# Layer 0 of a two-layer transformer kernel: the chain that prepares the FFN input starts half a batch earlier

## The chip, the cores and the metric

One NeuronCore of a Trainium2 chip runs the whole program. The metric is the device time of one execution in microseconds (us). The engines are TensorE (PE: matrix products and transposes; PEld is its weight load), VectorE (DVE), ScalarE (ACT), GpSimd (POOL) and the queues that issue DMAs (SP). Each runs its own instruction list in order, and semaphores are the only thing that ties the lists together.

## The reference

Input `x` is 16 batches x 256 positions x 256 features in fp32. Four steps follow one another, each added to `x`:

```python
x = x + tanh(g_xattn[0]) * L0_xattn(layernorm(x), ctx, ctx)   # decayed running sum of ctx*ctx, times layernorm(x)
x = x + tanh(g_ffn[0])   * L0_ffn(layernorm(x), w_gate, w_up, w_down)
x = x + tanh(g_xattn[1]) * L1_xattn(layernorm(x), ctx, ctx, 16)   # softmax attention with RoPE and ALiBi
x = x + tanh(g_ffn[1])   * L1_ffn(layernorm(x), w_fc, b_fc, w_proj, b_proj)
```

The change touches the first two. `L0_ffn` quantises both operands of every product to FP4 in blocks of 16 along the contracted dimension (scale = max|x|/6, value rounded to the grid 0, 0.5, 1, 1.5, 2, 3, 4, 6, times scale): `gate = q(y) q(Wg)^T`, `up = q(y) q(Wu)^T`, `h = silu(gate) * up`, `out = q(h) q(Wd)^T`, with 256 features and 704 hidden.

## The kernel before

Everything of layer 0 stays in SBUF. A batch is 256 rows, held as 2 tiles of 128 partitions, and each engine runs one `l0_body(b)` for each of the 16 batches (`over_batches`: bodies 0 to 3 and 12 to 15 are written out, 4 to 11 are a hardware loop of two bodies). The order of every engine's list is written by hand in that engine's `l0_body`. The bodies are software-pipelined: body b does the gate/up product of batch b, the down product of batch b-1 (`prv`), the last preparation of batch b+1 (`nxt`), and earlier work of b+2 to b+4 (`nxt2` is b+2).

**The y chain** makes the quantised FFN input of a batch n from the residual `xres` after its first update:
`l0_x_mix` (DVE, `mix`) and `l0_x_sum` (POOL, `xres += mix`); `l0_y_stats` (DVE, mean and variance); `l0_ln_step` (POOL, four tiny operations to `shift`; the same call serves the statistics of batch b+4); `l0_y_norm` (ACT, `yn`); `l0_y_scale` (DVE: maximum of each block L1287, a small scalar operation L1279 and reciprocal L1281, to `yrinv`); `l0_y_scaled` (POOL, `ys`, L1096); `l0_y_magic` (ACT, magnitude `ymag`); `l0_y_round` (DVE, `yup` then `ycode`); `l0_y_quantised` (POOL, `yq`, L1103); `l0_turn_input` (PE, four transposes into PSUM `ps_r`, L471); `l0_input_out` (ACT, `yth`, L837); `l0_y_low` (DVE, `ytl`, L1301).

**The h chain** of batch b: `l0_gate_up` (PE: four units u0 to u3 of 12 matmuls, L491 to L493, into two pairs of banks of `ps_gu`); after each unit `l0_silu` (ACT) and `l0_multiply` (DVE, `h`, L1311; called mul0 to mul3 below). Unit u2 overwrites the banks of u0 and waits for mul0, u3 waits for mul1. Then `l0_hidden_scale` (DVE: L1318, L1279, L1281, to `hrinv`), `l0_hidden_scaled` (POOL, `hs`, L1110), `l0_hidden_magic` (ACT, `hmag`, L866), and in the next body `l0_hidden_up` and `l0_hidden_codes` (DVE, `hup` L1324 and `hcode` L1330) and `l0_hidden_quantised` (POOL, `hq`, L1116), whose result PE transposes in four groups (`l0_turn_hidden`, L510; ACT copies each, `l0_hidden_out`) and multiplies (`l0_down`, L522). `l0_add_ffn` (DVE, L1334) adds the result to the residual.

PE ends a body with `l0_decayed_sum(b+3)` (L460 to L462), which writes `ps_r` as `l0_turn_input` does, so the two take turns with `l0_x_mix` and `l0_y_low`. In body 0 DVE also quantises W_down (`w_scale` to `w_dequant`) and PE transposes it (`turn_w2`).

Of the kernel before, what the change touches and what calls it, by code (L numbers as in the profile page):

```python
# [145 lines left out]
def build_main(nc, load, loaded, out_v, g_xattn, g_ffn, w_gate_up, w_down, w_fc, b_fc, w_proj, b_proj, ident, decay,  # L146
# [3 lines left out]
    with ExitStack() as keep:  # L150
# [262 lines left out]
        def _(pe):  # L413
# [112 lines left out]
            def l0_hidden_out(b, nxt):  # L526
                l0_turn_hidden(b, 0)
                l0_turn_hidden(b, 1)
                l0_down(b, 0)
                l0_turn_hidden(b, 2)  # L530
                l0_down(b, 1)
                if nxt:
                    l0_turn_input(nxt)
                l0_turn_hidden(b, 3)
                l0_down(b, 2)
                l0_down(b, 3)
# [244 lines left out]
        def _(act):  # L781
# [86 lines left out]
            def l0_body(b):  # L868
                prv = b.shifted(-1)
                l0_silu(b, 0)  # L870
                if b.shifted(1):
                    l0_y_norm(b.shifted(1))
                l0_silu(b, 1)
                if b.shifted(3):
                    l0_x_norm(b.shifted(3))
                l0_silu(b, 2)
                if b.shifted(1):
                    l0_y_magic(b.shifted(1))
                l0_silu(b, 3)
                if prv:  # L880
                    l0_hidden_out(prv, 0)
                    l0_hidden_out(prv, 1)
                else:
                    w_magnitude(W2)
                if b.shifted(4):
                    l0_square(b.shifted(4))
                if prv:
                    l0_hidden_out(prv, 2)
                if b.shifted(1):
                    l0_input_out(b.shifted(1))  # L890
                if prv:
                    l0_hidden_out(prv, 3)
                else:
                    for k in range(KH0 // 2):
                        w2_out(k)
                l0_hidden_magic(b)

# [131 lines left out]
            l0_square(fourth)  # L1029
            l0_input_out(first)  # L1030
            over_batches(act, l0_body, L0_AHEAD, L0_BEHIND)

            at_v_of(first)
# [18 lines left out]
        def _(pool):  # L1052
# [66 lines left out]
            def l0_body(b):  # L1119
# [7 lines left out]
                if b.shifted(1):  # L1127
                    l0_y_scaled(b.shifted(1))
                if b.shifted(2):
                    l0_x_sum(b.shifted(2))  # L1130
                if b.shifted(1):
                    l0_y_quantised(b.shifted(1))
                l0_hidden_scaled(b)
                if b.shifted(2):
                    l0_ln_step(b.shifted(4), b.shifted(2))

# [81 lines left out]
            l0_y_scaled(first)  # L1218
            l0_y_quantised(first)
            v_aug_rows = a_v_aug[:, :, :, :, :].rearrange("p a c h s -> p (a c h) s")  # L1220
            nc.gpsimd.memset(v_aug_rows[:, :, HD + 1:2 * HD], 0.0)
# [24 lines left out]
        def _(dve):  # L1246
# [90 lines left out]
            def l0_body(b):  # L1337
# [6 lines left out]
                l0_multiply(b, 0)  # L1344
                if nxt:
                    l0_y_scale(nxt)
                l0_multiply(b, 1)
# [3 lines left out]
                if nxt2:  # L1351
                    l0_x_mix(nxt2)
                l0_multiply(b, 2)
                if b.shifted(4):
                    l0_x_stats(b.shifted(4))
                l0_multiply(b, 3)
                if nxt:
                    l0_y_round(nxt)
                l0_hidden_scale(b)
                if not prv:  # L1360
                    w_up(W2)
                    w_round(W2)
                    w_dequant(W2)
                if nxt:
                    l0_y_low(nxt)
                if nxt2:
                    l0_y_stats(nxt2)
                if prv:
# [279 lines left out]
            for k in range(len(w1_turns)):  # L1648
                if k == 4:
                    l0_y_round(first)  # L1650
                w1_low(k)
            l0_y_low(first)
            over_batches(dve, l0_body, L0_AHEAD, L0_BEHIND)

# [91 lines left out]
```

## Time and profile before

| | |
|---|---|
| three runs, device time | 862.52, 864.06, 865.29 us; median 864.06 |
| the profiled execution | 860.4 us, of which the span from first to last instruction is 858.4 us |
| layer 0 loop over batches | about 46 us to 343 us of the span |
| busy share over the span | PE 82%, DVE 82%, ACT 57%, POOL 52% |
| of the stretch 180 to 220 us (40 us) | PE 37.83, DVE 32.70, ACT 18.93, POOL 26.39 us busy |

Durations come from the one profiled execution. The overlap of two neighbours on one engine is real: an instruction may start up to 0.1 us before the recorded end of the one ahead. "[0.74 <-DVE h L1311]" behind a row is the engine's idle time before that instruction and who ended it.

### The profile page before, as it was taken

The numbers are of one execution on the slowest core, as the hardware profiler recorded it, in microseconds if no ns is written. First come the engines' busy times: TensorE is split into PE (matmuls) and PEld (weight loads), VectorE is DVE, ScalarE is ACT, GpSimd is POOL, SyncE is SP. The second block draws the span as 40 slices with busy tenths as digits, with TensorE's granted clock in tenths as the row PEclk, the third lists the DMA queues.
The fourth block names the chain that finished last, engine by engine and source line by source line (L and its number), as shares of the span: only waits on it lengthen the run. The fifth ranks groups of instructions, "written<-read, shape, count | busy, mean of one in ns | idle before, by whom it ended". The sixth has DMA issues, their size and how long they took to land.

```text
span 858.4 us, 16548 instructions
## 1 busy us (share of the span) xinstructions
PE 708.2 (82%) x5075; PEld 511.9 (60%) x5090; DVE 702.6 (82%) x1230; ACT 487.1 (57%) x939; POOL 445.0 (52%) x331
## 2 busy tenths in 40 slices
PE   2357999999999998779999999999999775777776
PEld 1246888887878876555665655566566443444444
DVE  6767888888878878868888988888888748898985
ACT  3334444544444442328777777777777684555653
POOL 4523666665666545744444455454542525565563
PEclk9877999999999999879999999999999997898999
DMA  8700000000000000010000000000001000010011
GB/s 277 226 26 0 1 1 1 0 0 0 0 0 1 1 1 1 1 48 5 3 2 2 1 1 1 1 1 1 1 1 50 2 2 0 26 37 24 26 37 50
DMA packets 17719, 18.35 MB, mean 21 GB/s; under 512 B 1670, under 2 KB 16912, under 8 KB 17680
## 3 DMA queue, kind: packets, MB, share of 16 engines
q1 hardware_dynamic: 17084, 17.66, 6.3%
q8 instruction: 21, 0.34, 0.2%
q10 hardware_dynamic: 596, 0.20, 0.1%
q14 instruction: 18, 0.15, 0.1%
HBM read 13.39 MB, written 4.19 MB: 20 GB/s over the span
## 4 chain that ended last, share of the span: by engine, by line
PE 44%; DVE 26%; issue 13%; ACT 9%; POOL 4%; DMA 1%; DVEq 1%; ACTq 0%; POOLq 0%; SPq 0%
PE ps_o L522 9%; PE a_ps_t L561 7%; PE a_ps_m L579 6%; DVE maxima L1499 5%; PE a_ps_pv L615 4%; DVE f_ps_small L1584 4%; PE a_ps_s L600 3%; PE ps_gu L491 2%; DVE yscale L1279 2%; DVE f_hcode L1600 2%; PE ps_gu L493 2%; PE ps_gu L492 2%; PE a_ps_pv L623 1%; ACT yn L830 1%; ACT probs L920 1%
## 5 line engine op out<-in xcount | busy, mean ns | idle before, releaser
L1499 DVE TENSOR_REDUCE maxima<-a_ps_m 128x2 f32<-128x512 f32 x256 | 166.4, 686 | 35.4 <-PE a_ps_m L579 34.7
L920 ACT ACTIVATE probs<-a_ps_s 128x512 f32<-128x512 f32 x256 | 149.1, 601 | 42.3 <-PE a_ps_s L600 39.5
L579 PE MATMUL a_ps_m<-stack_t 64*128 64x256 f32 x512 | 107.6, 328 | 19.7 <-DVE maxima L1499 16.6
L579 PEld LDWEIGHTS a_ps_m<-stack_t 64*128 64x128 f32 x512 | 68.2, 188 | 78.6 <-DVE maxima L1499 49.4
L1142 POOL TENSOR_TENSOR stack<-roped,stack 128x512 f32<-128x512 f32 x32 | 42.7, 1334 | 116.9 <-DVE stack L1489 115.4
L600 PE MATMUL a_ps_s<-stack_t 64*128 64x256 f32 x512 | 100.0, 308 | 3.7 <-ACT probs L920 2.8
L522 PE MATMUL ps_o<-w2t,hqt 128*128 128x256 f32 (+1 forms) x384 | 99.1, 392 | 4.6 <-ACT hqt L851 4.6
L491 PE MATMUL ps_gu<-w1h,yth 128*128 128x352 f32 x256 | 87.5, 342 | 14.1 <-DVE h L1311 14.1
L615 PE MATMUL a_ps_pv<-probs,v_aug 128*32 128x256 f32 x1024 | 83.0, 396 | 2.9 <-ACT probs L920 2.5
L911 ACT CAST stack_t<-a_ps_t 128x512 fp32r<-128x512 f32 x128 | 70.9, 588 | 24.7 <-PE a_ps_t L561 23.8
L561 PE MATMUL a_ps_t<-idf,stack 128*128 128x128 f32 x512 | 77.3, 294 | 9.3 <-POOL stack L1142 4.9
L492 PE MATMUL ps_gu<-w1l,yth 128*128 128x352 f32 x256 | 82.7, 323 | 0.0
L493 PE MATMUL ps_gu<-w1h,ytl 128*128 128x352 f32 x256 | 82.5, 322 | 0.0
L522 PEld LDWEIGHTS ps_o<-w2t,hqt 128*128 128x128 f32 (+1 forms) x384 | 66.3, 189 | 25.5 <-issue 13.4
L600 PEld LDWEIGHTS a_ps_s<-stack_t 64*128 64x128 f32 x512 | 68.5, 187 | 12.8 <-ACT probs L920 6.6
L843 ACT ACTIVATE sg<-ps_gu 128x352 f32<-128x352 f32 x64 | 29.7, 465 | 76.6 <-PE ps_gu L493 76.6
L561 PEld LDWEIGHTS a_ps_t<-idf,stack 128*128 128x128 f32 x512 | 58.9, 148 | 22.4 <-ACT stack_t L911 8.2
L1191 POOL TENSOR_TENSOR f_hup<-f_h,f_hmag 128x2048 f32<-128x2048 f32 x16 | 58.3, 3642 | 10.5 <-DVE f_hcode L1600 9.5
L491 PEld LDWEIGHTS ps_gu<-w1h,yth 128*128 128x128 f32 x256 | 48.2, 188 | 20.2 <-DVE h L1311 19.1
L1116 POOL TENSOR_TENSOR hq<-hcode,hscale 128x1408 f32<-128x1408 bf16 x16 | 41.5, 2596 | 35.6 <-DVE hcode L1330 35.6
L981 ACT ACTIVATE f_h<-f_ps_fc 128x512 f32<-128x512 f32 x64 | 36.1, 596 | 37.9 <-POOL f_hup L1191 35.5
L1110 POOL TENSOR_TENSOR hs<-h,hrinv 128x1408 f32<-128x1408 f32 x16 | 42.7, 2668 | 22.9 <-DVE hrinv L1281 22.9
(176 smaller groups left out, 1589.4 us busy)
## 6 DMA issues: line engine op xcount, KB each, us to landing
xres<-in_x SPq DMA_DIRECT2D x16, 256.0 KB, 3.1
ctx<-in_ctx SPq DMA_DIRECT2D x16, 256.0 KB, 4.0
out_x<-f_y SPq DMA_DIRECT2D x16, 256.0 KB, 2.1
w1a_raw<-in_w_gate_up SPq DMA_DIRECT2D x1, 1024.0 KB, 5.9
w_raw<-in_w_fc SPq DMA_DIRECT2D x1, 1024.0 KB, 5.4
w_raw<-in_w_proj SPq DMA_DIRECT2D x1, 1024.0 KB, 5.0
w_raw<-in_w_down SPq DMA_DIRECT2D x1, 704.0 KB, 9.2
stack_t<-neg_max_t SPq DMA_DIRECT2D x32, 8.0 KB
```

The source lines that it names most:

```text
L491: nc.tensor.matmul(into, yth[:, kc, c, :], w1h[:, kc, cols], start=kc == 0, stop=False)
L492: nc.tensor.matmul(into, yth[:, kc, c, :], w1l[:, kc, cols], start=False, stop=False)
L493: ins = nc.tensor.matmul(into, ytl[:, kc, c, :], w1h[:, kc, cols], start=False, stop=kc == KD - 1)
L522: ins = nc.tensor.matmul(ps_o[:, c, :], hqt[0:rows, g, n, :], w2t[0:rows, k, :], start=k == 0, stop=k == KH0 - 1)
L561: ins = nc.tensor.transpose(a_ps_t[:, g % 2, (n * C + c) * P:(n * C + c + 1) * P], a_stack[:, b.par, which, c, 2 * pair:2 * pair + 2, :].r ...
L579: ins = nc.tensor.matmul(a_ps_m[:, half, n, :], a_stack_t[b.par][rows, 0, pair, c * P:(c + 1) * P], a_stack_t[b.par][rows, 1, pair, :], st ...
L600: ins = nc.tensor.matmul(a_ps_s[:, half, n, :], a_stack_t[b.par][rows, 1, pair, kc * P:(kc + 1) * P], a_stack_t[b.par][rows, 0, pair, :], ...
L615: ins = nc.tensor.matmul(a_ps_pv[32 * n:32 * n + 32, quad % 2, 0:T], a_v_aug[:, b.par, kc, 4 * quad + n, :], a_probs[:, (2 * g + n % 2) % ...
L911: nc.scalar.copy(a_stack_t[b.par][:, g % 2, pair:pair + 2, :].rearrange("p a t -> p (a t)"), a_ps_t[:, g % 2, :]).then_inc(a_t, 1)
L920: nc.scalar.activation(a_probs[:, u % 8], a_ps_s[:, u % 2], ACT.Exp).then_inc(a_exp, 1)
L1191: nc.gpsimd.tensor_tensor(f_blocks(f_hup[:, :]), f_blocks(f_h[:, b.par]), f_spread(f_hmag[:, b.par], F_NBH), ALU.add).then_inc(f_g_hup, 1)
L1499: nc.vector.tensor_reduce(a_maxima[:, b.par, c, 4 * quad + half:4 * quad + half + 3:2], a_ps_m[:, half], X, ALU.max).then_inc(a_v_max, 1)
```

## The change

In words, by engine, for body b:

- **VectorE**: `l0_y_scale` goes from behind mul0 (for b+1) to just ahead of `l0_add_ffn` (for b+2). `l0_y_round(b+1)` goes from behind mul3 to behind `l0_x_mix`, ahead of mul2. `l0_y_stats(b+2)` goes from behind `l0_y_low` to behind mul3, ahead of `l0_hidden_scale`.
- **GpSimd**: `l0_y_scaled` goes from behind `hq` (for b+1) to the end of the body (for b+2); `l0_y_quantised(b+1)` goes ahead of `l0_x_sum(b+2)`; `l0_ln_step` goes ahead of `l0_hidden_scaled`.
- **ScalarE**: `l0_y_norm` goes from behind the first silu (for b+1) to ahead of `l0_hidden_magic` (for b+2); `l0_y_magic(b+1)` goes from behind the third silu to the head of the body; `l0_x_norm` and `l0_square` shift by a place; `l0_input_out(b+1)` goes ahead of the third hidden copy.
- **TensorE**: `l0_turn_input(b+1)` goes from behind the second down group to behind the second transpose group.
- Batch 1's norm, scale and scaling, which body 0 did, are now done ahead of the loop.

```diff
--- before.py
+++ after.py
@@ -526,11 +526,11 @@
             def l0_hidden_out(b, nxt):
                 l0_turn_hidden(b, 0)
                 l0_turn_hidden(b, 1)
+                if nxt:
+                    l0_turn_input(nxt)
                 l0_down(b, 0)
                 l0_turn_hidden(b, 2)
                 l0_down(b, 1)
-                if nxt:
-                    l0_turn_input(nxt)
                 l0_turn_hidden(b, 3)
                 l0_down(b, 2)
                 l0_down(b, 3)
@@ -867,32 +867,31 @@
 
             def l0_body(b):
                 prv = b.shifted(-1)
+                if b.shifted(1):
+                    l0_y_magic(b.shifted(1))
                 l0_silu(b, 0)
-                if b.shifted(1):
-                    l0_y_norm(b.shifted(1))
-                l0_silu(b, 1)
                 if b.shifted(3):
                     l0_x_norm(b.shifted(3))
+                l0_silu(b, 1)
                 l0_silu(b, 2)
-                if b.shifted(1):
-                    l0_y_magic(b.shifted(1))
                 l0_silu(b, 3)
                 if prv:
                     l0_hidden_out(prv, 0)
                     l0_hidden_out(prv, 1)
                 else:
                     w_magnitude(W2)
+                if b.shifted(1):
+                    l0_input_out(b.shifted(1))
                 if b.shifted(4):
                     l0_square(b.shifted(4))
                 if prv:
                     l0_hidden_out(prv, 2)
-                if b.shifted(1):
-                    l0_input_out(b.shifted(1))
-                if prv:
                     l0_hidden_out(prv, 3)
                 else:
                     for k in range(KH0 // 2):
                         w2_out(k)
+                if b.shifted(2):
+                    l0_y_norm(b.shifted(2))
                 l0_hidden_magic(b)
 
             def at_v_of(b):
@@ -1028,6 +1027,7 @@
                 w1_high(k)
             l0_square(fourth)
             l0_input_out(first)
+            l0_y_norm(second)
             over_batches(act, l0_body, L0_AHEAD, L0_BEHIND)
 
             at_v_of(first)
@@ -1125,14 +1125,13 @@
                     at_rstd(first)
                     at_q_parts(first)
                 if b.shifted(1):
-                    l0_y_scaled(b.shifted(1))
+                    l0_y_quantised(b.shifted(1))
                 if b.shifted(2):
                     l0_x_sum(b.shifted(2))
-                if b.shifted(1):
-                    l0_y_quantised(b.shifted(1))
+                    l0_ln_step(b.shifted(4), b.shifted(2))
                 l0_hidden_scaled(b)
                 if b.shifted(2):
-                    l0_ln_step(b.shifted(4), b.shifted(2))
+                    l0_y_scaled(b.shifted(2))
 
             def at_low_part(b, which):
 
@@ -1217,6 +1216,7 @@
             l0_ln_step(fourth, second)
             l0_y_scaled(first)
             l0_y_quantised(first)
+            l0_y_scaled(second)
             v_aug_rows = a_v_aug[:, :, :, :, :].rearrange("p a c h s -> p (a c h) s")
             nc.gpsimd.memset(v_aug_rows[:, :, HD + 1:2 * HD], 0.0)
             nc.gpsimd.memset(v_aug_rows[:, :, HD:HD + 1], 1.0).then_inc(a_v_aug_laid, 1)
@@ -1342,29 +1342,27 @@
                     l0_hidden_up(prv)
                     l0_hidden_codes(prv)
                 l0_multiply(b, 0)
-                if nxt:
-                    l0_y_scale(nxt)
                 l0_multiply(b, 1)
                 if not prv:
                     w_scale(W2)
                     w_times(W2)
                 if nxt2:
                     l0_x_mix(nxt2)
+                l0_y_round(nxt)
                 l0_multiply(b, 2)
                 if b.shifted(4):
                     l0_x_stats(b.shifted(4))
                 l0_multiply(b, 3)
-                if nxt:
-                    l0_y_round(nxt)
+                if nxt2:
+                    l0_y_stats(nxt2)
                 l0_hidden_scale(b)
                 if not prv:
                     w_up(W2)
                     w_round(W2)
                     w_dequant(W2)
-                if nxt:
-                    l0_y_low(nxt)
+                l0_y_low(nxt)
                 if nxt2:
-                    l0_y_stats(nxt2)
+                    l0_y_scale(nxt2)
                 if prv:
                     l0_add_ffn(prv)
 
@@ -1650,6 +1648,7 @@
                     l0_y_round(first)
                 w1_low(k)
             l0_y_low(first)
+            l0_y_scale(second)
             over_batches(dve, l0_body, L0_AHEAD, L0_BEHIND)
 
             dve.wait_ge(t_gu, last.count(4, 4))
```

TensorE, body 2, the place between the transposes of the hidden codes and the down product (`yq` is the input that is turned, `hq` the hidden codes):

```order
 L510 MATMUL ps_tb<-idf,hq 128x128 x2
 L510 MATMUL ps_tb<-idf,hq 64x128
-L522 MATMUL ps_o<-w2t,hqt 128x256 x3
-L510 MATMUL ps_ta<-idf,hq 128x128 x3
-L522 MATMUL ps_o<-w2t,hqt 128x256 x3
 L471 MATMUL ps_r<-idf,yq 128x128 x4
+L522 MATMUL ps_o<-w2t,hqt 128x256 x3
+L510 MATMUL ps_ta<-idf,hq 128x128 x3
+L522 MATMUL ps_o<-w2t,hqt 128x256 x3
 L510 MATMUL ps_tb<-idf,hq 128x128 x2
```

The four transposes of `yq` now stand ahead of the first two down groups.

VectorE before, from the hidden rounding of the batch behind to the second multiply pair of body 2 (`h` is a multiply, `yscale` and `yrinv` the y scale, `mix` the x mix):

```order
L1324 SCALAR_TENSOR_TENSOR hup<-hmag,hs 128x1408
L1330 SCALAR_TENSOR_TENSOR hcode<-hmag,hup 128x1408
L1311 TENSOR_TENSOR h<-sg,ps_gu 128x352
L1287 TENSOR_REDUCE yscale<-yn 128x32
L1279 TENSOR_SCALAR yscale<-yscale 128x32
L1281 RECIPROCAL yrinv<-yscale 128x32
L1311 TENSOR_TENSOR h<-sg,ps_gu 128x352
L1269 SCALAR_TENSOR_TENSOR mix<-ps_r,gates,xn 128x512
L1311 TENSOR_TENSOR h<-sg,ps_gu 128x352
L1250 BN_STATS stats<-xres 128x6 x2
L1257 BN_AGGR mv<-stats 128x2 x2
L1311 TENSOR_TENSOR h<-sg,ps_gu 128x352
```

VectorE of the changed kernel, the same place:

```order
L1324 SCALAR_TENSOR_TENSOR hup<-hmag,hs 128x1408
L1330 SCALAR_TENSOR_TENSOR hcode<-hmag,hup 128x1408
L1311 TENSOR_TENSOR h<-sg,ps_gu 128x352 x2
L1269 SCALAR_TENSOR_TENSOR mix<-ps_r,gates,xn 128x512
L1293 SCALAR_TENSOR_TENSOR yup<-ymag,ys 128x512
L1297 SCALAR_TENSOR_TENSOR ycode<-ymag,yup 128x512
L1311 TENSOR_TENSOR h<-sg,ps_gu 128x352
L1250 BN_STATS stats<-xres 128x6 x2
L1257 BN_AGGR mv<-stats 128x2 x2
L1311 TENSOR_TENSOR h<-sg,ps_gu 128x352
L1250 BN_STATS stats<-xres 128x6 x2
```

The y scale no longer stands between the first and the second multiply, the y rounding stands ahead of the third, and a second pair of statistics stands behind the fourth.

GpSimd before, one body from `hq` on (`ys` is the scaled and `yq` the quantised input, `var` to `shift` the ln step, `hs` the scaled hidden):

```order
L1116 TENSOR_TENSOR hq<-hcode,hscale 128x1408
L1096 TENSOR_TENSOR ys<-yn,yrinv 128x512
L1090 TENSOR_TENSOR xres<-xres,mix 128x512
L1103 TENSOR_TENSOR yq<-ycode,yscale 128x512
L1110 TENSOR_TENSOR hs<-h,hrinv 128x1408
L1080 TENSOR_TENSOR var<-mv,eps 128x4
L1082 TENSOR_TENSOR rstd<-var,pow_half 128x4
L1084 TENSOR_TENSOR neg_rstd<-rstd,minus_one 128x4
L1086 TENSOR_TENSOR shift<-mv,neg_rstd 128x4
```

GpSimd of the changed kernel, the same body:

```order
L1116 TENSOR_TENSOR hq<-hcode,hscale 128x1408
L1103 TENSOR_TENSOR yq<-ycode,yscale 128x512
L1090 TENSOR_TENSOR xres<-xres,mix 128x512
L1080 TENSOR_TENSOR var<-mv,eps 128x4
L1082 TENSOR_TENSOR rstd<-var,pow_half 128x4
L1084 TENSOR_TENSOR neg_rstd<-rstd,minus_one 128x4
L1086 TENSOR_TENSOR shift<-mv,neg_rstd 128x4
L1110 TENSOR_TENSOR hs<-h,hrinv 128x1408
L1096 TENSOR_TENSOR ys<-yn,yrinv 128x512
```

`ys` went to the end, `yq` ahead of the sum, and the ln step ahead of `hs`.

## Rows read from the trace of the kernel before

**Rows 1.** Waits of all engines, 100 to 320 us: total, times, longest.

```profile
PE ps_gu L491 <- DVE h L1311: 9.2, 13, 0.9
```

**Rows 2.** Timeline of one batch, all engines: start, us, engine, line, operation [idle before].

```profile
183.44 1.63 DVE L1324 SCALAR_TENSOR_TENSOR hup<-hmag,hs 128x1408 f32<-128x1408 bf16 x1 [0.16 <-ACT hmag L866]
...
185.10 1.62 DVE L1330 SCALAR_TENSOR_TENSOR hcode<-hmag,hup 128x1408 bf16<-128x1408 bf16 x1
...
186.16 1.08 ACT L830 ACTIVATE yn<-xres,shift,rstd 128x256 f32 x2
...
186.89 2.60 POOL L1116 TENSOR_TENSOR hq<-hcode,hscale 128x1408 f32<-128x1408 bf16 x1 [1.76 <-DVE hcode L1330]
...
188.00 1.52 DVE L1279 TENSOR_SCALAR yscale<-yscale 128x32 f32<-128x32 f32 x1
...
189.56 0.35 DVE L1281 RECIPROCAL yrinv<-yscale 128x32 f32<-128x32 f32 x1
...
190.34 0.43 PE L491 MATMUL ps_gu<-w1h,yth 128*128 128x352 f32 x1 [0.74 <-DVE h L1311]
...
191.15 1.30 POOL L1090 TENSOR_TENSOR xres<-xres,mix 128x512 f32 x1
...
193.07 0.52 DVE L1311 TENSOR_TENSOR h<-sg,ps_gu 128x352 f32<-128x352 f32 x1 [0.70 <-ACT sg L843]
...
193.46 1.56 PE L522 MATMUL ps_o<-w2t,hqt 128*128 128x256 f32 x6 [0.27 <-ACT hqt L851]
193.51 0.69 DVE L1293 SCALAR_TENSOR_TENSOR yup<-ymag,ys 128x512 f32<-128x512 bf16 x1
...
194.23 0.69 DVE L1297 SCALAR_TENSOR_TENSOR ycode<-ymag,yup 128x512 bf16<-128x512 bf16 x1
...
194.84 1.61 DVE L1318 TENSOR_REDUCE hscale<-h 128x88 f32<-128x1408 f32 x1
...
195.08 1.06 POOL L1103 TENSOR_TENSOR yq<-ycode,yscale 128x512 f32<-128x512 bf16 x1 [2.62 <-DVE ycode L1297]
...
196.73 0.70 DVE L1281 RECIPROCAL hrinv<-hscale 128x88 f32<-128x88 f32 x1
...
196.77 0.65 PE L471 MATMUL ps_r<-idf,yq 128*128 128x128 f32 x4
...
197.51 2.59 POOL L1110 TENSOR_TENSOR hs<-h,hrinv 128x1408 f32<-128x1408 f32 x1 [1.36 <-DVE hrinv L1281]
...
198.69 0.74 DVE L1250 BATCH_NORM_STATS2 stats<-xres 128x6 f32 x2
199.35 0.41 DVE L1257 BATCH_NORM_AGGREGATE mv<-stats 128x2 f32<-128x6 f32 x2
...
200.13 1.38 ACT L866 ACTIVATE hmag<-hs 128x1408 bf16<-128x1408 f32 x1 [1.66 <-POOL hs L1110]
...
200.71 0.75 DVE L1334 SCALAR_TENSOR_TENSOR xres<-ps_o,gates,xres 128x512 f32 x1 [0.95 <-PE ps_o L522]
...
201.54 1.63 DVE L1324 SCALAR_TENSOR_TENSOR hup<-hmag,hs 128x1408 f32<-128x1408 bf16 x1
```

**Rows 3.** Timeline of VectorE in the first bodies of the loop over batches.

```profile
55.96 0.74 DVE L1269 SCALAR_TENSOR_TENSOR mix<-ps_r,gates,xn 128x512 f32<-128x512 f32 x1
...
59.77 1.61 DVE L1318 TENSOR_REDUCE hscale<-h 128x88 f32<-128x1408 f32 x1
...
74.42 1.63 DVE L1324 SCALAR_TENSOR_TENSOR hup<-hmag,hs 128x1408 f32<-128x1408 bf16 x1 [3.41 <-ACT hmag L866]
```

**Rows 4.** Timeline of ScalarE in the first body of that loop.

```profile
73.00 1.38 ACT L866 ACTIVATE hmag<-hs 128x1408 bf16<-128x1408 f32 x1
```

**Rows 5.** Timeline of VectorE: the hidden rounding before bodies 14 and 15.

```profile
310.63 1.62 DVE L1324 SCALAR_TENSOR_TENSOR hup<-hmag,hs 128x1408 f32<-128x1408 bf16 x1 [0.21 <-ACT hmag L866]
...
328.63 2.53 DVE L1324 SCALAR_TENSOR_TENSOR hup<-hmag,hs 128x1408 f32<-128x1408 bf16 x1 [0.21 <-ACT hmag L866]
```

**Rows 6.** Timeline of GpSimd at the same place as the second row above.

```profile
328.39 1.29 POOL L1150 TENSOR_TENSOR part_sin<-ctx,sin 128x512 f32<-128x512 f32 x1
```

## The prediction

> **What bounds the kernel now.** The page puts PE and DVE both at 82% busy over the span, so neither total decides; I went to the waits of the stretch in which layer 0 is steady, then to the timeline of one batch. The waits show PE idle for one thing that repeats: the first matmul of unit u3 waits for DVE's mul1, 13 times, 9.2 us in all [rows 1]. The timeline says why. I count from hup, the first step of a body, at 183.44 [rows 2]. hcode ends at 186.72, hq runs on GpSimd from 186.89 to 189.49. DVE's small scalar operation on the y scale is issued at 188.00 and ends at 189.52: 1.52 us for 32 numbers a partition, ending 0.03 after hq. It was held until GpSimd had finished. Behind it stand the reciprocal and mul1, so u3 starts at 190.34, and everything else follows: mul3 193.07, yup, ycode, hscale 194.84, hrinv until 197.43, hs until 200.10, hmag until 201.51, next hup 201.54. That closed chain, DVE, GpSimd, DVE, PE, DVE, GpSimd, ScalarE, is 18.10 us long. Over the 13 bodies from 74.42 to 310.63 the mean is 236.21 / 13 = 18.17 [rows 3, 5]. The question is what the chain becomes, and how long PE's own list is.
>
> **PE alone.** u3 would follow u2 at once, at 189.44 (0.16 a matmul); it came 0.90 later and its first step took 0.11 more, so 1.0 goes if mul1 is early. A down group waits 0.27 for its copy at 193.46 [rows 2]; the moved transposes fill that. PE's floor is about 18.2 - 1.0 - 0.25 = 16.95 us a body.
>
> **The new chain, one body, from hup = 0** [rows 2]. hcode ends at 3.28, hq at 6.05, as now. mul0, mul1 and x mix are done by about 5; the y rounding is then next on DVE. It reads two SBUF operands. The nearest row for such an operation beside GpSimd is the hup of body 15: issued at 328.63, with GpSimd busy until 329.68, it took 2.53 instead of 1.62 and ended 1.48 after GpSimd's end, 0.14 less than its own length [rows 5, 6]. So yup (0.69) ends at 6.05 + 0.55 = 6.60, ycode at 7.33 (0.72 behind yup's start plus 0.69, less what overlaps). yq starts 0.16 later, 7.49, and ends 8.55; the x sum follows it at 8.52 and takes 1.30: 9.82. The y statistics now stand ahead of hscale and wait for that sum. With the same 0.16 they start at 9.98 (mul3 is done by 9.2), and cost 0.66 + 0.34 to the next operation: hscale 10.98. Then as now: 2.59 to hrinv's end, 13.57; 0.08; hs 2.59, 16.24; hmag 0.03 + 1.38, 17.65; hup 17.68. The bound from the free side: without the hold yup would start near 5, yq would start at once when hq ends, and the chain would be 16.6, under PE's floor. From the other side: every hand-over 0.1 longer, 18.2.
>
> The rule behind the hold is stated by the Trainium skill, "SBUF — State Buffer", section Who interferes with whom: a VectorE instruction with two SBUF inputs contends with a GpSimd instruction that reads SBUF, and whoever issued first holds the port for its whole length. It speaks against this change, because the y rounding leaves a stretch in which GpSimd is idle. By that rule the sum is the one made here; if it did not hold for this pair, the time would be the third case below. The hup row agrees with it.
>
> **What hides the rest.** The ln step's four operations now stand ahead of hs on GpSimd. Statistics end at 11.05; the four take about 2.2, to 13.3, while hs waits for hrinv until 13.6: cover 0.3. `l0_y_norm` (1.08) now stands ahead of hmag on ScalarE: behind the last hidden copy, about 13.4 to 14.5, and hmag is wanted at 16.3: hidden. The y scale's scalar operation, beside hs, is held until hs ends, 16.27; reciprocal and add_ffn end by 17.5, before hup. `ys` runs 16.8 to 17.9, so hup is held by it by 0.06: 17.74. The transposes of yq start on PE at 8.6, where it is free at about 8.5; down0 follows at 9.1, and add_ffn may start 200.71 - 193.46 - 0.49 = 6.76 later, 15.9. PE's u2 waits about 0.5 for mul0 instead of u3 for mul1; its body is 17.7 too, 0.8 over its floor. `v_low` for the decayed sum comes at 14.2, PE wants it at 15.6. `l0_y_magic` at the head of ScalarE's body ends 0.65 after `ys`, at 18.6, and the first silu of that body is wanted at about 19. `l0_x_norm`, `l0_square` and `l0_input_out` shift under idle time.
>
> A period saves 18.10 - 17.74 = 0.36 in the loop and some 0.45 in written-out bodies, where the hand-over to yq is 0.08 shorter; I take 0.40. **Thirteen periods: -5.2.**
>
> **The start: +3.4.** Batch 1's norm, scale and scaling ahead of the loop lie in PE's first unit: free. In body 0 the x mix starts at 55.96 and hscale at 59.77 [rows 3]. Now behind the mix: yup 0.66, ycode 0.72, its end 0.69, yq 0.08 + 1.03, x sum 1.30, 0.14, statistics 1.0 = 5.6, so hscale comes at 61.6, 1.8 later; 0.3 comes back since mul1 no longer stands behind the y scale. All of W_down's preparation stands behind it, and hmag at 73.00 [rows 4] waits in the end for its transposes: +1.5. Then y norm, not hidden here, stands between those copies and hmag: +1.0. Then ys of batch 2 and the hidden rounding meet: hup gets the port, ys waits for it, hcode waits for ys: +0.9, the hold of the hup row.
>
> **The end: -1.6 and -0.85.** Body 14 has no y statistics, sum or scale. hscale follows mul3, hmag is done near 15.5, and add_ffn decides: yq ends at 8.4, transposes 8.45, down0 8.95, add_ffn 15.7, 0.75, hup 16.4 against 18.0 now (328.63 - 310.63 [rows 5]). And hup of body 15 lost 0.90 to `part_sin`; GpSimd now starts that pair when hs ends, 14.0, and is through at 16.55, so hup loses 0.06.
>
> **Sum:** 3.4 - 5.2 - 1.6 - 0.85 = -4.3 us. Against the profiled execution's 860.4 that is 856.1; the runs' median lies 3.7 above it, and the same step gives 864.06 - 4.3 = **859.8**. Behind layer 0 nothing changes, and the chain from mul3 of batch 15 into attention is the same.
>
> **Rivals.** *Cover gone, no gain*: the ln step ahead of hs, or longer hand-overs, put 0.4 into each chain. For it: 0.3 of cover is thin, and GpSimd's tiny operations are held by two-operand work. Against: hscale's reduction reads one operand. Periods as now leave 3.4 - 2.5: 865.0. Chance 0.23. *The hold does not apply to yup*: periods fall to PE's floor, 0.8 less each, 10.4 in all: 849.4. Against: the hup row. Chance 0.07. *Slower, the order of ys and hup turns round in every body*, as in body 0: if y norm ends so late that the y scale is not waiting when hs ends, hup takes the port first, ys waits, hcode waits for ys, 0.85 a body, 11.0 in all: 859.8 + 11.0 = 870.8. It decides from y norm ending 0.75 before hs ends plus another 0.86; y norm ends 1.7 before. Chance 0.12. The forecast has 0.58.
>
> **The numbers.** A measurement of this kernel tells about 0.3% (2.6 us) from no change. The forecast's own spread is 2.5 us either way (0.2 a period); about 0.07 of its chance lies within 0.3%. Faster 0.51 + 0.07 = 0.58, same 0.30, slower 0.12. The range takes in the forecast, start losses 1 less with periods 0.2 shorter (856.0), and the no-gain case up to 865.5; it leaves out 0.07 and 0.12.
>
> **What would show it.** Each step is right if the profile of the changed kernel shows: mul0 and mul1 together and no PE wait on mul1; yup over 0.9 us long and ending 0.55 after hq; yq right behind, and the second statistics idle for the x sum; period of hup near 17.7; hmag of body 0 about 2.5 later; hup before body 15 near 1.6 long. Wrong: hs waiting for the ln step, hmag for y norm, hcode 2.5 long, or PE waiting over 0.5 for yq.

## The result, and the profile after

| | median us | lowest to highest | ratio to before, 95% interval |
|---|---|---|---|
| before | 863.77 | 860.43 to 869.76 (14 runs) | |
| after | 860.12 | 856.69 to 863.96 (14 runs) | 0.9946 (0.9929 to 0.9963) |

The changed kernel is 0.54% faster, 3.65 us by the medians. A measurement of this kernel can tell about 0.3% from nothing, and the whole interval lies further from no change than that (0.37% at its upper end). The profiled execution of the changed kernel took 860.34 us (span 858.2), that of before 860.4 us. By this pair alone nothing was gained. The execution of before lay 3.4 us under its median and that of after lay on its own, so the traces have to be compared place by place.

Timeline of one batch of the changed kernel, all engines, from hup on (start, us, engine, line, operation [idle before]); it answers to [rows 2]:

```profile
184.89 1.63 DVE L1324 SCALAR_TENSOR_TENSOR hup<-hmag,hs 128x1408 f32<-128x1408 bf16 x1 [0.46 <-ACT hmag L866]
...
188.09 0.99 DVE L1311 TENSOR_TENSOR h<-sg,ps_gu 128x352 f32<-128x352 f32 x2
188.33 2.60 POOL L1116 TENSOR_TENSOR hq<-hcode,hscale 128x1408 f32<-128x1408 bf16 x1 [3.33 <-DVE hcode L1330]
188.66 0.43 PE L491 MATMUL ps_gu<-w1h,yth 128*128 128x352 f32 x1 [0.63 <-DVE h L1311]
...
189.66 1.82 DVE L1293 SCALAR_TENSOR_TENSOR yup<-ymag,ys 128x512 f32<-128x512 bf16 x1
...
191.51 0.69 DVE L1297 SCALAR_TENSOR_TENSOR ycode<-ymag,yup 128x512 bf16<-128x512 bf16 x1
...
192.36 1.06 POOL L1103 TENSOR_TENSOR yq<-ycode,yscale 128x512 f32<-128x512 bf16 x1 [1.43 <-DVE ycode L1297]
...
193.38 1.27 POOL L1090 TENSOR_TENSOR xres<-xres,mix 128x512 f32 x1
...
194.90 0.75 DVE L1250 BATCH_NORM_STATS2 stats<-xres 128x6 f32 x2 [0.83 <-POOL xres L1090]
...
195.91 1.62 DVE L1318 TENSOR_REDUCE hscale<-h 128x88 f32<-128x1408 f32 x1
...
198.66 2.59 POOL L1110 TENSOR_TENSOR hs<-h,hrinv 128x1408 f32<-128x1408 f32 x1 [0.74 <-DVE hrinv L1281]
...
200.04 1.25 DVE L1279 TENSOR_SCALAR yscale<-yscale 128x32 f32<-128x32 f32 x1
...
201.28 1.38 ACT L866 ACTIVATE hmag<-hs 128x1408 bf16<-128x1408 f32 x1 [2.00 <-POOL hs L1110]
...
202.69 1.68 DVE L1324 SCALAR_TENSOR_TENSOR hup<-hmag,hs 128x1408 f32<-128x1408 bf16 x1 [0.45 <-ACT hmag L866]
```

The reader is to see four things. The two multiplies now stand together, and u3 has no wait. yup takes 1.82 us where its row in [rows 2] has 0.69: hq ends at 190.93 and yup at 191.48, 0.55 later. Behind ycode everything is one after another: yq, the x sum, the second statistics (idle 0.83 for that sum), hscale. And the small scalar operation on the y scale is still held: it takes 1.25 us and ends at 201.29, 0.04 after hs. But it now lies beside hs and nobody waits for it, except that `ys` starts late and hup takes 1.68 instead of 1.63. This body takes 17.80 us against 18.10.

Waits of all engines of the changed kernel, 100 to 320 us (engine, line, waited for: total us, times, longest), beside [rows 1]:

```profile
POOL yq L1103 <- DVE ycode L1297: 18.3, 13, 1.4
...
DVE stats L1250 <- POOL xres L1090: 9.7, 12, 0.8
...
PE ps_gu L491 <- DVE h L1311: 8.6, 12, 1.7
```

PE's total for its multiply is nearly what it was (9.2 before), but it is another wait: u2 for mul0, 0.63 in the row at 188.66. That is slack, for the chain is now bound elsewhere: in e2 below, where yup is not held, PE's wait over 200 us is 1.8 instead of 6.8.

By the starts of hup, with those of before behind them: body 1 at 77.17 (74.42), body 2 at 95.98 (92.43), body 14 at 309.44 (310.63), body 15 at 325.61 (328.63), the last rounding, behind body 15, at 346.84 (349.17). So the start costs, each period returns 0.4, and the last two bodies go their own way:

VectorE of the changed kernel, body 1 and body 15; GpSimd for the same two places ([rows 5, 6] of before):

```profile
77.17 1.63 DVE L1324 SCALAR_TENSOR_TENSOR hup<-hmag,hs 128x1408 f32<-128x1408 bf16 x1
78.83 2.37 DVE L1330 SCALAR_TENSOR_TENSOR hcode<-hmag,hup 128x1408 bf16<-128x1408 bf16 x1
...
309.44 1.63 DVE L1324 SCALAR_TENSOR_TENSOR hup<-hmag,hs 128x1408 f32<-128x1408 bf16 x1 [0.45 <-ACT hmag L866]
...
325.61 2.03 DVE L1324 SCALAR_TENSOR_TENSOR hup<-hmag,hs 128x1408 f32<-128x1408 bf16 x1
...
337.83 0.52 DVE L1311 TENSOR_TENSOR h<-sg,ps_gu 128x352 f32<-128x352 f32 x1 [2.10 <-ACT sg L843]
```

```profile
77.27 2.45 POOL L1096 TENSOR_TENSOR ys<-yn,yrinv 128x512 f32<-128x512 f32 x1 [9.23 <-DVE yrinv L1281]
...
324.86 1.30 POOL L1149 TENSOR_TENSOR part_sin<-ctx,sin 128x512 f32<-128x512 f32 x1
```

In body 1, hup is issued 0.10 ahead of `ys` and runs at its own length; `ys` (own length 1.06) runs until 79.72, and hcode, issued meanwhile, takes 2.37 instead of 1.62. In body 15 hup ends 1.48 after `part_sin`, as in [rows 5, 6].

### The profile page after: what moved, and what is told of

Same layout as the page of the kernel before. It is cut to its first block, busy times and chain, and to the rows that moved or that the text cites. A ratio compares the mean times of both kernels' runs of the same rounds, so it can differ in the third digit from the quotient of the medians.

```text
span 858.2 us, 16571 instructions
## 1 busy us (share of the span) xinstructions
PE 713.5 (83%) x5090; PEld 517.0 (60%) x5090; DVE 708.5 (83%) x1230; ACT 488.0 (57%) x939; POOL 431.1 (50%) x331
## 4 chain that ended last, share of the span: by engine, by line
PE 33%; DVE 30%; issue 16%; POOL 9%; ACT 8%; DVEq 1%; DMA 1%; POOLq 1%; ACTq 0%; SPq 0%
PE a_ps_t L561 7%; PE a_ps_m L579 6%; DVE maxima L1497 5%; PE a_ps_pv L615 4%; DVE f_ps_small L1582 4%; PE a_ps_s L600 3%; POOL hs L1110 3%; PE ps_o L522 3%; DVE hup L1324 2%; DVE f_hcode L1598 2%; DVE yup L1293 2%; POOL xres L1090 2%; DVE hscale L1318 2%; ACT hmag L866 1%; PE a_ps_pv L623 1%
## 5 line engine op out<-in xcount | busy, mean ns | idle before, releaser
L703 PE MATMUL f_ps_h<-idb,f_hcode 128*128 128x128 bf16 x256 | 25.9, 261 | 33.6 <-DVE f_hcode L1598 33.5
```

## The experiments

Each is an edit of the kernel before or of the changed one, and e6 is two of them together. The first four ran beside 29 runs of before (median 864.05), the second four beside 23 (median 863.7).

| kernel | edit | median us | ratio to before, 95% interval |
|---|---|---|---|
| e1_before_no_hold | before, small operation on 33 numbers in another split | 864.02 | 0.9997 (0.9974 to 1.0020) |
| e2_after_ymag_psum | after, `ymag` in PSUM | 852.63 | 0.9884 (0.9852 to 0.9916) |
| e3_after_no_hold | after, the edit of e1 | 860.55 | 0.9955 (0.9934 to 0.9975) |
| e4_after_turn_back | after, input transposes at their old place | 859.91 | 0.9951 (0.9933 to 0.9969) |
| e5_after_norm_early | after, y norm ahead of W_down's copies in body 0 | 857.15 | 0.9937 (0.9914 to 0.9959) |
| e6_psum_and_norm_early | e2 and e5 | 853.25 | 0.9870 (0.9832 to 0.9907) |
| e7_before_scale_from_psum | before, small operation reads its maximum from PSUM | 848.59 | 0.9829 (0.9799 to 0.9859) |
| e8_sum_before_yq | after, x sum ahead of `yq` | 861.83 | 0.9986 (0.9955 to 1.0018) |

### Is the held operation the whole cost of the old order?

The theory: before loses 1.0 us a body to one held operation of 32 numbers, and the new order wins by moving it out of PE's way. Then the old order without the hold must do better than the new one. The first edit tried for that changes the shape of the small operation: 33 numbers come in as one row of 33 and go out as 11 rows of 3, so that the outermost counts of source and destination are odd and differ:

```diff
-                nc.vector.tensor_reduce(yscale[:, b.par], blocks(flat(yn[:, b.par])), X, ALU.max,
+                nc.vector.tensor_reduce(yamax[:, 0:NBY], blocks(flat(yn[:, b.par])), X, ALU.max,
...
+                out = yscale[:, b.par].rearrange("p (a c) -> p a c", a=11)
+                nc.vector.tensor_scalar(out, yamax[:, :], 1.0 / 6.0, 1e-12, ALU.mult, ALU.max).then_inc(v_yscale, 1)
```

> The kernel before, in its own order; only the y scale's small scalar operation is written so that its input and output are split differently (33 numbers in, 11 x 3 out), so that it should not need the port that GpSimd holds. Hold theory (what the change bought is that this operation no longer waits for hq between mul0 and mul1): the operation takes about 0.2 us instead of 1.5, PE's wait for mul1 (0.74) goes, and the period of hup falls from 18.18 us to PE's floor with the input transposes at their old place, about 17.2; 13 periods give some 13 us, time about 851, faster than the changed kernel. Rival (the half-batch lead of the y chain is what pays): the chain stands where it stood, so time within 2 us of before. If the other split does not avoid the hold, the operation stays at 1.5 us and the run says nothing on either.

> The changed kernel with the same edit of the y scale's small operation as in the run on the kernel before. Chain theory (the hold of this operation, about 1.1 us a body beside hs, lies beside work that decides): the operation falls to 0.2, the period stays at 17.79 less at most 0.06, time within 1 us of the changed kernel. Rival (each hold on VectorE costs its length wherever it stands): 1.0 us less in each of 13 bodies, about 847.

Measured: 0.9997 and 0.9955, what their parents have. VectorE of e1, then GpSimd, in the body of [rows 2], show why (its lines are numbered a little higher):

```profile
188.02 1.50 DVE L1282 TENSOR_SCALAR yscale<-yamax 128x33 f32<-128x33 f32 x1
```

```profile
186.89 2.60 POOL L1118 TENSOR_TENSOR hq<-hcode,hscale 128x1408 f32<-128x1408 bf16 x1 [1.75 <-DVE hcode L1339]
```

The operation on 33 numbers is held as the one on 32 was, until 189.52, 0.03 after hq. In e3 it takes 1.25 us beside hs. The edit did not take the hold away, so neither run tests the theory: both are inconclusive. The row shows 33 numbers on both sides. The 11 rows of 3 lie next to each other in memory, so it stays open whether the engine treated the two sides as different or as one row of 33 each. The Trainium skill, "VectorE: DVE Perf Modes", section Mode 2×_2P, gives as a condition of the mode that uses both read ports that the outermost dimension that is not 1 be even, or odd and equal on both sides. The split built from it did not avoid the hold, 1.50 us against 0.19 in the row of e7 below. No run here bears that condition out, and none refutes it, since the two sides may have been equal after all.

The edit that does take it away puts the maximum of each block into the PSUM bank `ps_ta`, which PE's hidden transposes use later in the body, and reads it from there. The waits added keep that bank free: VectorE waits until ScalarE has copied the third hidden group, the last that uses this bank, and PE's first transpose waits for the small operation.

```diff
+                if b.shifted(-3):
+                    dve.wait_ge(a_ht, b.shifted(-3).count(4, 3))
...
-                nc.vector.tensor_reduce(yscale[:, b.par], blocks(flat(yn[:, b.par])), X, ALU.max,
+                nc.vector.tensor_reduce(ps_ta[:, 0:NBY], blocks(flat(yn[:, b.par])), X, ALU.max,
...
+                nc.vector.tensor_scalar(yscale[:, b.par], ps_ta[:, 0:NBY], 1.0 / 6.0, 1e-12, ALU.mult, ALU.max).then_inc(v_yscale, 1)
...
+                if g == 0 and b.shifted(2):
+                    pe.wait_ge(v_yscale, upto(V_SCALE, b.shifted(2), "scale"))
```

> The kernel before, in its own order; the block maximum of the y scale goes to the PSUM bank ps_ta and the small operation (L1279's work) reads it there, so that it has one operand outside SBUF. Hold theory (all that the changed order bought is that this operation no longer holds up mul1): it takes about 0.2 us instead of 1.5, PE's wait for mul1 goes, the period of hup falls from 18.18 to PE's floor with the old place of the transposes, about 17.2, and layer 0 ends some 13 us earlier: about 851, well under the changed kernel. Rival (the half-batch lead of the y chain is what pays): within 2 us of before. If the operation is still held, nothing is said on either.

Measured: 848.59 us, 0.9829, the lowest median of all kernels here. VectorE of e7, then GpSimd of the same stretch:

```profile
177.93 1.63 DVE L1334 SCALAR_TENSOR_TENSOR hup<-hmag,hs 128x1408 f32<-128x1408 bf16 x1 [0.17 <-ACT hmag L869]
...
181.85 0.70 DVE L1294 TENSOR_REDUCE ps_ta<-yn 128x32 f32<-128x512 f32 x1 [0.21 <-ACT yn L833]
182.59 0.19 DVE L1297 TENSOR_SCALAR yscale<-ps_ta 128x32 f32<-128x32 f32 x1
182.81 0.35 DVE L1299 RECIPROCAL yrinv<-yscale 128x32 f32<-128x32 f32 x1
183.08 0.46 DVE L1321 TENSOR_TENSOR h<-sg,ps_gu 128x352 f32<-128x352 f32 x1
...
195.02 1.63 DVE L1334 SCALAR_TENSOR_TENSOR hup<-hmag,hs 128x1408 f32<-128x1408 bf16 x1
```

```profile
181.38 2.60 POOL L1119 TENSOR_TENSOR hq<-hcode,hscale 128x1408 f32<-128x1408 bf16 x1 [1.76 <-DVE hcode L1340]
```

The same 32 numbers take 0.19 us, in the middle of hq, and mul1 follows at 183.08. PE goes from u2 to u3 without a wait. Bodies 1 to 14 take (298.39 - 74.65) / 13 = 17.21 us each against 18.17, and the last hup stands at 335.81 against 349.17. Layer 0 ends 13.4 us earlier in the trace, and the medians are 15.1 us apart, where about 13 was expected. Only the place of these 32 maxima was changed, with the waits that keep the bank free; the operation's place in the list and hq's are the same. So it is shown that the hold, and with it the 1 us a body, comes from this operand lying in SBUF. That what the two engines contend for is a port is what the prediction took from the Trainium skill; it fits, and no run looks at the port itself.

### What did the new order leave on the table?

The theory: the new order exchanges the hold of the small operation for one of yup, and with it has 0.4 of 1.0 us a body. In the changed kernel `ymag`, one of yup's two SBUF inputs, is put into PSUM. It becomes fp32 with that; yup's own length stays as it was, 0.68 us:

```diff
-        ymag = low("ymag", [P, C * D], BF16)
...
+        ymag = ps_ta
...
+                if g == 0 and b.shifted(2):
+                    pe.wait_ge(v_yround, upto(V_ROUND, b.shifted(2), "codes"))
```

> The changed kernel with ymag in the PSUM bank ps_ta instead of SBUF, so that yup and ycode read one SBUF operand; PE's first hidden transposes wait for ycode. Hold theory (the chain of the changed kernel is hq, held yup, ycode, yq, x sum, y statistics): yup takes 0.7 us instead of 1.8, ycode ends before hq, yq starts right behind hq, the chain shrinks by about 1.4 to some 16.5 and PE's floor of about 16.95 to 17.0 becomes the period of hup (17.79 now); time about 9 to 10 us below the changed kernel, near 850.5. Rival (the yq that stands behind hq on GpSimd, or PE's new wait, keeps the period): the hold goes but the time stays within 2 us of the changed kernel.

Measured: 852.63 us, 0.9884. VectorE, then GpSimd of e2:

```profile
185.65 0.68 DVE L1296 SCALAR_TENSOR_TENSOR yup<-ps_ta,ys 128x512 f32<-128x512 f32 x1
...
189.77 0.76 DVE L1253 BATCH_NORM_STATS2 stats<-xres 128x6 f32 x2 [0.32 <-POOL xres L1093]
```

```profile
183.96 2.59 POOL L1119 TENSOR_TENSOR hq<-hcode,hscale 128x1408 f32<-128x1408 bf16 x1 [3.33 <-DVE hcode L1333]
...
187.22 1.06 POOL L1106 TENSOR_TENSOR yq<-ycode,yscale 128x512 f32<-128x512 bf16 x1 [0.67 <-DVE ycode L1300]
```

yup starts and ends within hq at its own 0.68. From the hup of body 2 to that of body 14 a body takes (300.92 - 94.31) / 12 = 17.22 us, as in e7. So both orders come to the same period once the operation that stands beside hq reads PSUM, and that period is nearly PE's list alone: from 100 to 300 us PE waits 1.8 in all in e2, for the multiplies, and 3.8 in e7, for ScalarE's copies. The move itself then buys nothing in the steady part, and in the traces its dearer start is what is left: hup of body 2 stands at 94.31 against 91.65, the last hup at 337.79 against 335.81. The medians say 852.6 against 848.6, but they come from different sets of runs and the two intervals touch, so this difference is less sure than the period.

### The position of the transposes

```diff
-                if nxt:
-                    l0_turn_input(nxt)
                 l0_down(b, 0)
                 l0_turn_hidden(b, 2)
                 l0_down(b, 1)
+                if nxt:
+                    l0_turn_input(nxt)
```

ScalarE's copy of them goes back with them.

> The changed kernel with the input transposes of PE and their copy on ScalarE put back where they were (behind the second down group). Chain theory (the period is the VectorE-GpSimd-ScalarE chain of 17.79, PE has 0.8 us of slack in it): a wait of 0.27 for the first hidden copy comes back on PE and the period stays at 17.8; time within 1 us of the changed kernel. Rival (filling PE's wait with the transposes is part of the gain): 0.3 to 0.5 us more in each body, 4 to 6 us, near 865.

Measured: 859.91 us, 0.9951 against 0.9946. The period is (309.42 - 96.06) / 12 = 17.78. PE waits for its copy again, and it costs nothing that shows. Waits of e4, 100 to 300 us:

```profile
PE ps_o L522 <- ACT hqt L851: 3.6, 11, 0.4
PE ps_gu L491 <- DVE h L1312: 3.2, 8, 0.5
```

The second row says where it went: u2 waits 3.2 us in all for mul0 and the down product 3.6 for the copy, 6.8 together. In the same 200 us PE of the changed kernel waits 6.8 for mul0 and not for the copy. PE has slack in this order, and filling one gap opens the next.

### The start

```diff
                 if prv:
                     l0_hidden_out(prv, 2)
                     l0_hidden_out(prv, 3)
-                else:
-                    for k in range(KH0 // 2):
-                        w2_out(k)
                 if b.shifted(2):
                     l0_y_norm(b.shifted(2))
+                if not prv:
+                    for k in range(KH0 // 2):
+                        w2_out(k)
```

> The changed kernel; in body 0 alone ScalarE does the y norm of batch 2 ahead of the copies of the turned W_down instead of behind them. Start theory (of the 3.5 us that the start loses, 1.0 is this norm ahead of hmag and 0.75 is hcode held by ys): hmag of body 0 starts at about 74.8 instead of 75.8, hcode takes 1.62 instead of 2.37, and body 1 is earlier by 1.75; the time falls by 1.5 to 2 us, to about 858.3. Rival (W_down's preparation alone sets the start): no change.

Measured: 857.15 us. Its ratio is 0.9937 against 0.9946, 0.8 us, and the intervals overlap, though the medians lie 2.97 apart. VectorE of e5, and GpSimd:

```profile
76.13 1.63 DVE L1324 SCALAR_TENSOR_TENSOR hup<-hmag,hs 128x1408 f32<-128x1408 bf16 x1 [3.21 <-ACT hmag L866]
77.79 1.63 DVE L1330 SCALAR_TENSOR_TENSOR hcode<-hmag,hup 128x1408 bf16<-128x1408 bf16 x1
```

```profile
73.00 1.06 POOL L1096 TENSOR_TENSOR ys<-yn,yrinv 128x512 f32<-128x512 f32 x1 [5.02 <-DVE yrinv L1281]
```

hup is 1.04 earlier and hcode is no longer held, 1.78 us together: the two terms that the prediction gave as 1.0 and 0.9. By the second hup it is 2.4 (93.58 against 95.98); the other 0.6 is a loss of PE's clock in body 1 of the changed kernel's execution, told below, which e5's execution does not have. The trace shows that; the time of the whole kernel is only compatible with it.

The same edit on e2 (e6 is e2 with the diff above, and a wait of batch 2's `l0_y_magic` for W_down's copies, which use the same bank):

> ymag in PSUM and the early y norm of body 0 together, on the changed kernel. If both are separate terms of the sum: 852.6 less 1.5 to 2, about 851, with hup of body 1 at about 75 and a period of 17.2 as with ymag in PSUM alone. If the early norm's gain is taken back by PE's clock or by the first bodies: 852.6.

Measured: 853.25 us, 0.9870 against e2's 0.9884: no difference that can be told. The hup of body 1 was expected near 75 and came at 77.55, later than e2's 76.69. The trace says why: this execution entered the loop late. Its x mix of body 0 stands at 57.29, ahead of everything that the edit touches, where e2's stands at 55.44. Counted from that x mix, hup of body 2 comes after 36.87 us against 38.87 in e2, and the last hup after 279.80 against 282.35. So within the loop the early norm gives about 2 us in this order too, and what the profiled execution lost was lost ahead of the loop. That the median does not fall stays unexplained: there are six runs of each, and their intervals are wider than the gain.

### A lever against the new hold that keeps all in SBUF

If yup's hold is the new bound, GpSimd could use that time: the x sum, which waits for nothing, ahead of `yq`.

```diff
+                if b.shifted(2):
+                    l0_x_sum(b.shifted(2))
                 if b.shifted(1):
                     l0_y_quantised(b.shifted(1))
                 if b.shifted(2):
-                    l0_x_sum(b.shifted(2))
                     l0_ln_step(b.shifted(4), b.shifted(2))
```

> The changed kernel with the x sum ahead of yq on GpSimd. Port theory (the one that waits gets the port when it comes free): yup, waiting, goes at hq's end, the x sum waits for yup, ycode then waits for the x sum, so ycode is about 1.9 us long, yq starts 1.1 later than now and the period grows by about 0.3, to 18.1; time about 4 us above the changed kernel. Rival (the x sum, right behind hq, is over before yq could start anyway and the y statistics come 0.8 earlier): period about 17.0 to 17.2 and some 8 us less.

Measured: 861.83 us, 0.9986, where the changed kernel has 0.9946: some 3.5 us more by the ratios, with intervals that overlap. The period is (310.38 - 96.38) / 12 = 17.83 against 17.79. VectorE of e8, then GpSimd:

```profile
191.52 0.88 DVE L1294 SCALAR_TENSOR_TENSOR yup<-ymag,ys 128x512 f32<-128x512 bf16 x1
192.44 1.66 DVE L1298 SCALAR_TENSOR_TENSOR ycode<-ymag,yup 128x512 bf16<-128x512 bf16 x1
...
195.88 0.74 DVE L1251 BATCH_NORM_STATS2 stats<-xres 128x6 f32 x2
```

```profile
189.26 2.60 POOL L1116 TENSOR_TENSOR hq<-hcode,hscale 128x1408 f32<-128x1408 bf16 x1 [3.31 <-DVE hcode L1331]
191.81 1.73 POOL L1090 TENSOR_TENSOR xres<-xres,mix 128x512 f32 x1
194.26 1.06 POOL L1103 TENSOR_TENSOR yq<-ycode,yscale 128x512 f32<-128x512 bf16 x1 [0.71 <-DVE ycode L1298]
```

The port changes hands: hq, yup (the x sum waits 0.4), the x sum (ycode waits 1.0), ycode. The second statistics no longer wait for the x sum, which would have given 0.8. But the 1.0 that ycode is held pushes mul2, the first statistics and mul3 back on VectorE, and the second statistics stand behind them: they start 10.07 after hup against 10.01 in the changed kernel, and hscale 11.07 against 11.02. The two cancel. `yq` starts 1.0 later after hup, 8.45 against 7.47, and PE waits about 1.0 a body for it, but the chain to the next hup does not go through it. So the steps of the port theory came as written (ycode 1.66 for 1.9, `yq` 1.0 later for 1.1) and its growth of the period to 18.1 did not; the rival's 17.2 did not come either.

## Why the prediction was right

The time was forecast as 859.8 and is 860.1, the change -4.3 and is -3.65 by the medians. The mechanism was right: the hold leaves mul1, yup gets it, and the chain through `yq`, the x sum and the statistics is the new period. That the time came within 0.3 us is luck in part, since 14 runs of the changed kernel spread over 7 us and single terms missed by up to 1.2, in both directions. By its own terms, counted from the starts of hup:

- **The chain of a body.** Forecast 17.74 for a body that took 18.10 before, and 0.40 saved a period; that body takes 17.80, and the mean over twelve periods is (309.44 - 95.98) / 12 = 17.79, 0.39 less than before ((310.63 - 92.43) / 12 = 18.18). The mean mixes two kinds: the bodies of the hardware loop went from 18.27 to 17.94 (forecast 0.36 less), the written-out ones from 18.01 to 17.50 (forecast 0.45 less). Its steps hold one by one, counted from hup = 0: hq ends at 6.04 (6.05), yup at 6.59 (6.60), `yq` starts at 7.47 (7.49), the x sum ends at 9.76 (9.82), statistics 10.01 (9.98), hscale 11.02 (10.98), hs ends 16.36 (16.24), hup 17.80 (17.74). This is what e2 confirms: take yup's hold away and the period falls to nearly PE's list.
- **The hold of yup** was taken from one row, hup beside `part_sin`, and came out as written: 0.55 after hq. The Trainium skill, "SBUF — State Buffer", section Who interferes with whom, states that a VectorE instruction with two SBUF inputs contends with a GpSimd instruction that reads SBUF; the trace agrees, 1.82 us beside hq against 0.69. In e2, where one of yup's inputs lies in PSUM, it takes 0.68 in the middle of hq.
- **The start**, forecast +3.4: hup of body 1 comes 2.75 later and hcode is held 0.75, 3.50 together. But body 1 itself returns nothing where 0.4 was in the sum: hup of body 2 is 3.55 late. PE's windows say why (us, busy of each engine (instructions), granted clock, DMA share, GB/s). Of the changed kernel, where the matmuls of u2 are recorded at 0.49 us each and not at 0.32:

```profile
78.00:81.00 3.00, 1.84 (x12) 1.55 (x10) 2.97 (x2) 1.25 (x3) 1.72 (x1) 1.00 0.00 0
81.00:84.00 3.00, 2.32 (x8) 2.32 (x9) 2.54 (x5) 1.06 (x3) 2.59 (x1) 0.65 0.00 0
84.00:87.00 3.00, 3.00 (x16) 3.00 (x16) 2.19 (x5) 0.46 (x1) 1.78 (x2) 0.78 0.00 0
```

  The granted clock went from full (2.4 GHz) to the lower level (1.2 GHz) for part of these stretches; before has 1.00 in all three. PE had stood idle for some 1.2 of 3 us, since the late hcode holds up mul0. The executions of e3 and e4 have the same hold of hcode and the full clock in these stretches, and their body 1 takes 18.16 us where the changed kernel's takes 18.81: 0.65 is what the clock cost here. Without it body 1 returns 0.6: 18.16 less the 0.75 of hcode, already counted, is 17.41, against 18.01 before.
- **Period 14**, forecast -1.6 (16.4 against 18.0): 325.61 - 309.44 = 16.17, -1.83.
- **hup of body 15**, forecast -0.85, held by 0.06: it takes 2.03, so -0.50, held by 0.40. The mechanism was right and the size was not: `part_sin` ended 0.17 later than I had put it and hup came 0.23 earlier, and the two are 0.4 together. The same rule, the end 1.48 after GpSimd's, gives 327.64, where it ended.
- **Not in the sum:** from mul0 to mul3 of body 15 before took 7.41 us, after takes 8.61. PE's granted clock fell again, in the changed kernel:

```profile
327.00:330.00 3.00, 2.16 (x14) 1.87 (x13) 2.96 (x4) 0.93 (x2) 0.62 (x1) 1.00 0.01 3
...
333.00:336.00 3.00, 2.10 (x9) 2.10 (x10) 2.62 (x8) 0.00 (x0) 0.89 (x2) 0.75 0.00 0
336.00:339.00 3.00, 2.81 (x13) 2.45 (x12) 1.14 (x2) 1.37 (x4) 2.32 (x2) 0.68 0.00 0
```

  and of the kernel before, where it stays at 1.00:

```profile
333.00:336.00 3.00, 2.19 (x12) 1.90 (x12) 2.97 (x4) 0.46 (x1) 2.49 (x1) 1.00 0.00 0
336.00:339.00 3.00, 1.58 (x10) 1.58 (x11) 2.87 (x11) 0.00 (x1) 0.70 (x1) 1.00 0.00 0
```

  But e1, whose order and whose rows up to here are those of the kernel before, has the loss too. Its mul0 to mul3 of body 15 take 8.96 us (332.69 to 341.65):

```profile
336.00:339.00 3.00, 1.62 (x6) 1.62 (x7) 2.86 (x11) 0.00 (x0) 0.70 (x1) 0.76 0.00 0
339.00:342.00 3.00, 2.77 (x14) 2.43 (x12) 0.56 (x2) 0.85 (x3) 2.52 (x2) 0.67 0.01 3
```

  So these 1.20 us are an accident of the execution and not a price of the new order. Without the loss the new order takes from mul0 to mul3 what the old one does, 7.41 us in e5 (326.86 to 334.27).

The terms of the trace add to 3.50 + 0.05 - 4.74 - 1.83 - 0.50 + 1.20 = -2.32 at the end of layer 0 (last hup -2.33). In the other two profiled executions of the new order without another gain, e3 and e4, the last hup stands at 345.75 and 345.61, -3.4 and -3.6, and -3.65 by the medians fits these. But the old order varies as well: in e1 the last hup stands at 350.66, 1.5 behind that of before. A single trace tells the end of layer 0 no better than that. Behind layer 0 the execution of the changed kernel lost what was left (clock 0.83 in 700 to 800 us and 0.92 after, against 0.85 and 0.96). That is the execution and need not be the change, which touches nothing there: from the last hup to the end of the span the old order takes 509.2 us in before and 514.0 in e1, the new one 511.4, 508.5 in e3 and 512.7 in e4.

Of the rivals, *cover gone* was wrong: hs waits for hrinv and not for the ln step, which ends at 197.91, 0.75 ahead of hs. *The hold does not apply* was wrong by yup's row. Its price can be read from e2, which makes it so: 849.4 by that rival, 852.6 measured. The gain is less since the period comes to 17.22 and not to PE's floor of 16.95. The moved transposes were to fill the wait for the copy, 0.33 a body in e7. In e2 that wait is gone, but PE waits 0.16 a body for its multiplies, and by an estimate from these waits its own list is 17.06 us long (17.22 - 0.16) where e7's is 16.88 (17.21 - 0.33). Why it is longer is open. *The order of ys and hup turns round* happened in body 1, as forecast, and in no other body.

One part of my reading was too narrow. I compared the new order only with the old one and took the held operation as a fact of the place. The larger gain, four times as much by the medians (15.1 against 3.65), was in its operand. Whether the moved transposes would add anything to that kernel was not tested.

## What to carry to other kernels

If a tiny VectorE operation has a row many times its own length (here 1.52 us against 0.19) that ends together with a GpSimd instruction, suspect that it is held: first change where it reads from (a PSUM bank that is free at that time, with the waits to keep it so) and only then reorder. Before moving a chain away from a hold, write down which VectorE operation will stand beside that GpSimd instruction next, look in the trace for one like it that was held, and give it the GpSimd end plus its own length; here that gave the new body to 0.06 us. And price the first and last body of a pipelined loop by themselves: here the start took back 3.5 of the 4.7 us that twelve periods gave. And before a few us between two traces are put down to a change, look at a second execution of the same order.

## What the hardware showed that I had not expected

- The small operation is held with 32 numbers (1.52 us) and with 33 (1.50), and not with its input in PSUM (0.19). An odd count did not leave the form that contends. Nothing in the code makes it wait for hq, so the lists of VectorE and GpSimd are tied together by more than semaphores.
- Behind hq the port goes to the engine that waits, and then back: hq, yup, x sum (1.73 instead of 1.29), ycode (1.66 instead of 0.69) in e8; hup, `ys` (2.45 instead of 1.06), hcode (2.37 instead of 1.63) in body 1. In these rows an engine did not keep the port for its next instruction while the other one waited.
- A held VectorE operation ends a little less than its own length after the release: yup 0.55 after hq (own 0.69), hup 1.48 after `part_sin` (own 1.62), hcode of body 1 1.48 after `ys` (own 1.62), each time 0.14 less.
- PE's granted clock fell inside layer 0 in two places behind idle time of PE (0.65 and 0.68 in stretches of 3 us). The same list of instructions at the same place kept 1.00 in one execution (before, PE busy 1.58 of 3) and fell to 0.76 in another (e1, 1.62 of 3), so what sets it off is open here. It took 0.65 and 1.2 us of a gain of 4 in the profiled execution.
